# Turning the q of four attention layers with transposing DMAs in place of matmuls

## What is computed

```python
x = x + _L0_attn_ref(_layernorm(x), ...)               # a state space layer, "m" below
x = x + _L0_xattn_ref(_layernorm(x), ctx, ctx, ...)    # cross attention, 16 heads of 8, "x0"
x = x + _L0_ffn_ref(_layernorm(x), ...)                # latent attention, 16 heads of 4, "s0", then 8 experts, top 2
x = x + _L1_attn_ref(_layernorm(x), ...)               # self attention, 4 key heads, "s1"
x = x + _L1_xattn_ref(_layernorm(x), ctx, ctx, ...)    # cross attention with rotation, "x1"
x = x + _L1_ffn_ref(_layernorm(x), ...)                # gelu MLP, "f"
```

## Time and profile before

| | |
|---|---|
| median of 3 runs | 752.23 us (751.91 to 753.66) |
| the profiled execution | 759.68 us |
| its span, first to last instruction | 757.9 us |
| mean granted TensorE clock | 0.98 |
| PE busy | 650.6 us (86%), 5800 matmul records |
| DVE busy | 557.3 us (74%), 1513 |
| ACT busy | 436.7 us (58%), 861 |
| POOL busy | 178.8 us (24%), 348 |

### The profile page before, as it was taken

One profiled execution on the slowest core, in us unless ns is written; L12 is line 12 of the kernel. 1 busy time (PEld: TensorE's weight loads), 2 busy tenths in 40 slices (PEclk: granted clock), 3 DMA queues, 4 the chain that ended last, 5 costly groups with the idle time before them and its releaser, 6 DMA issues.

```text
span 757.9 us, 14898 instructions
## 1 busy us (share of the span) xinstructions
PE 650.6 (86%) x5800; PEld 428.1 (56%) x5800; DVE 557.3 (74%) x1513; ACT 436.7 (58%) x861; POOL 178.8 (24%) x348
## 2 busy tenths in 40 slices
PE   0787889899899898898988898888899799898877
PEld 0255448547555585456743585555567467584556
DVE  8549885847986679786787557789858875669683
ACT  0423565676577546756476543646775677657634
POOL 9332430203212022321131103232311301020102
PEclk9979999999999999999999998989999999999999
DMA  8110000000000000000000000000000000000000
GB/s 288 49 65 8 1 1 1 1 2 1 1 14 10 1 2 15 8 2 1 10 6 1 2 1 15 1 2 1 1 15 2 1 1 1 1 1 1 2 1 22
DMA packets 10358, 10.62 MB, mean 14 GB/s; under 512 B 2832, under 2 KB 9520, under 8 KB 10032
## 3 DMA queue, kind: packets, MB, share of 16 engines
q1 hardware_dynamic: 9568, 6.98, 3.1%
q10 hardware_dynamic: 720, 2.69, 0.9%
HBM read 8.60 MB, written 1.07 MB: 13 GB/s over the span
## 4 chain that ended last, share of the span: by engine, by line
PE 53%; DVE 30%; ACT 10%; issue 4%; POOL 2%; POOLq 0%; ACTq 0%; DVEq 0%
PE psA L1551 8%; PE psB L1538 7%; PE psO L1489 7%; DVE qs L1139 7%; ACT P L840 6%; PE psB L1465 5%; PE psA L1449 4%; PE psM L1428 4%; DVE QT L1127 3%; PE psM L1304 2%; DVE qs L1134 2%; PE psM L1347 2%; DVE spare L1113 1%; PE psO L1480 1%; ACT QT L837 1%
## 5 line engine op out<-in xcount | busy, mean ns | idle before, releaser
L840 ACT ACTIVATE P<-psB 128x512 f32<-128x512 f32 x320 | 177.8, 596 | 105.3 <-PE psB L1465 69.2
L1139 DVE TENSOR_REDUCE qs<-psA 128x2 bf16<-128x512 f32 x256 | 165.0, 689 | 25.0 <-PE psA L1449 23.7
L1449 PE MATMUL psA<-kz_s,QT 128*128 128x512 bf16 x256 | 91.8, 391 | 13.3 <-DVE qs L1139 6.3
L847 ACT ACTIVATE P<-psB,W 128x256 f32<-128x256 f32 x160 | 66.9, 472 | 49.5 <-PE psB L1538 42.1
L1465 PE MATMUL psB<-QT,kz_s 128*128 128x256 bf16 x512 | 86.7, 276 | 5.3 <-ACT QT L837 4.4
L1489 PE MATMUL psO<-P,vp 128*32 128x256 f32 x1024 | 81.7, 393 | 6.8 <-ACT P L840 4.7
L1428 PE MATMUL psM<-identb,qs 128*128 128x128 bf16 x896 | 72.6, 222 | 13.9 <-DVE qs L1115 5.9
L1428 PEld LDWEIGHTS psM<-identb,qs 128*128 128x128 bf16 x896 | 56.3, 99 | 39.6 <-issue 13.4
L1465 PEld LDWEIGHTS psB<-QT,kz_s 128*128 128x128 bf16 x512 | 39.7, 98 | 52.9 <-issue 31.1
L1127 DVE COPY QT<-psM 128x1024 bf16<-128x1024 bf16 (+1 forms) x80 | 52.5, 660 | 19.7 <-PE psM L1428 18.8
L1551 PE MATMUL psA<-w,P 128*128 128x128 f32 x512 | 65.7, 278 | 0.6 <-DVE x L1216 0.4
(11 more groups left out here) (178 smaller groups left out, 1128.3 us busy)
## 6 DMA issues: line engine op xcount, KB each, us to landing
w<-expert_w ACTq DMA_DIRECT2D x2, 1024.0 KB, 8.7
toep<-decay_rows SPq DMA_DIRECT2D x4, 512.0 KB, 5.8
x<-x SPq DMA_DIRECT2D x8, 128.0 KB, 2.8
y<-base SPq DMA_DIRECT2D x8, 128.0 KB, 1.9
W<-weights SPq DMA_DIRECT2D x1, 940.0 KB, 6.6
rows<-bias_rows SPq DMA_DIRECT2D x1, 872.0 KB, 7.6
ctxp<-context SPq DMA_DIRECT2D x8, 64.0 KB, 2.1
fw<-mlp_w ACTq DMA_DIRECT2D x2, 256.0 KB, 10.6
```

The lines of the kernel that those rows point to most:

```text
L840: act.activation(P[:, p, :, :].rearrange("p a s -> p (a s)"), psB[:, s.u % B_BANKS, :], ACT.Exp, scale=LAYERS[s.L]["scale"]).then_inc(b_dr ...
L847: ins = act.activation(P[:, p, f, :], psB[:, s.u % B_BANKS, f * S:f * S + S], ACT.Gelu, bias=bias[:, n:n + 1])
L1139: dve.tensor_reduce(qs[L["W"]][j][:, t * H + h:t * H + h + 2, 0], ps.rearrange("p (h c) -> p h c", h=2), AX.X, ALU.max, negate=True).then_ ...
L1449: ins = pe.matmul(ps, QT[j][:, h // L["HB"], t * 128:t * 128 + 128], kz[s.L][j][:, kv:kv + 2, :].rearrange("p h s -> p (h s)"), start=True ...
```

## The change

The steps Q and M leave PE, DVE and ACT, and become steps of SP alone. SP gets its own order string and its own waits. For each turn it waits for `q_split` (Q) or `a_drained` (M) and issues two DMAs with transpose=True, one for each 128 positions, straight from `qs` to `QT`: [128, 512] bf16 to [128, 4, 128] (in s0 [128, 256] to [128, 2, 128]). PE waits before the first A or S of a half for the semaphore `q_turned` of that slot and half. The context loads, stores and x loads stand in SP's string as well. The strings of the other four engines are new too.

```diff
     if s.kind in ("Q", "M"):
-        return ("PE", "ACT") if query_on_scalar(s) else ("PE", "DVE")
+        return ("SP",)
...
-        "00w0102010010w101000a1a01a01aaaawa101101b0b10w1b02bb00b00a0b000b0001a001aa100a1aa100aaa0xaaa10aa1aa211aa1a1b1a"
...
+        "w00w0010100011121002001w1aaaaawa20110001102bb0abbb000b00000101001020aa001aaa1baaa0xaaa1aaa11aa1a11a1a1a1xaa1a1"
...
+    "SP": (
+        "00aa11bb00awa11b22b00ccaa020a121abbcx0c11bb33d2d12cc33dd22cc44e3e3yd24d4ee33dd344e55ef66fgg4455eeff664gg77hh57"
+        "57hfhf66g7g7hh55f66fg77ghh567"
...
+    turns = {}
+    for s in order["SP"]:
+        if s.kind in ("Q", "M"):
+            turns[s.j, s.q] = turns.get((s.j, s.q), 0) + 16 * T
+            s.turn = turns[s.j, s.q]
...
+        def query_turn(s, t):
 
             groups = groups_of(s)
-            n = len(groups)
-            return QT[s.j][:, groups[0]:groups[0] + n, :].rearrange("p g s -> p (g s)"), bf(m)[:, 0:n * S]
+            n, hb = len(groups), LAYERS[s.L]["HB"]
+            h = t * H + groups[0] * hb
+            return (QT[s.j][:, groups[0]:groups[0] + n, t * 128:t * 128 + 128],
+                    qs[LAYERS[s.L]["W"]][s.j][:, h:h + n * hb, :].rearrange("p h w -> p (h w)"))
...
-            for s in order["DVE"]:
-                if s.kind == "C" and s.L == "x1" and s.q == 0 and s.b + 2 < B:
+            for s in order["SP"]:
+                if s.kind == "C":
...
+                if s.kind in ("Q", "M"):
+                    if s.kind == "Q":
+                        split = previous(s, "P3", s.L).after["q_split"]
+                        if ahead(q_split, split):
+                            sp.wait_ge(q_split, split)
+                    else:
+                        a = previous(s, "A", s.L, 2 * s.q + 1 if LAYERS[s.L]["cross"] else 8 * s.q + 7).a
+                        if ahead(a_drained, a + 1):
+                            sp.wait_ge(a_drained, a + 1)
+                    for t in range(T):
+                        turned, plain = query_turn(s, t)
+                        sp.dma_start(turned, plain, transpose=True).then_inc(q_turned[s.j][s.q], 16)
...
-                if s.kind in ("Q", "M"):
-                    m = filled(s)
-                    dst, src = query_block(s, m)
-                    dve.tensor_copy(dst, src).then_inc(misc_drained[m], 1)
...
-                    drained(previous(s, "M", s.L, s.q // 2 if L["cross"] else s.q // 8))
+                    turned(previous(s, "M", s.L, s.q // 2 if L["cross"] else s.q // 8))
```

More of the change, by code:

```diff
@@ L133, in engines @@
     if s.kind in ("Q", "M"):
-        return ("PE", "ACT") if query_on_scalar(s) else ("PE", "DVE")
+        return ("SP",)
     if s.kind == "C":
-        return ("PE", "DVE") if s.q else ("PE", "DVE", "POOL")
+        return ("PE", "DVE") if s.q else ("PE", "DVE", "POOL", "SP") if s.L == "x1" and s.b + 2 < B else ("PE", "DVE", "POOL")
     if s.kind == "F3":
@@ L139, in engines @@
     if s.kind == "H":
-        return ("PE", "DVE") if s.L == "s0" else ("PE", "DVE", "POOL")
+        return ("PE", "DVE") if s.L == "s0" else ("PE", "DVE", "POOL", "SP")
     if s.kind == "R1":
@@ new lines @@
+        "0000000011120221b00b20bb0b2bbb1010120021111111111222111011100120x222222032322122311113x11331132322y321cccc11cc"
+        "1cc23232y3y212222222223222323223243343333333333343233223322y42222434334432dddddd422dd3423344233333333334334433"
+        "4343354444444444454444344333333334544543eeee33e3eee4554346z464444454446544464444646556655z66z46644545545554444"
+        "5555555565555566556456446466666z646666766576675576776775ffff7777ffff557577775557577777777555776755555656777767"
+        "gggg5gggg5655676677666667h66hh6hh5hhh766766766665777777777775775777765666556755776767667775755656676777567"
@@ L190 @@
-        "7675676757"
+        "0w1200101w0001111x222000022011002311x33y111223334y322244423324445333533454665z64z45554666447777557767667575666"
+        "7775556677"
+    ),
+    "SP": (
+        "00aa11bb00awa11b22b00ccaa020a121abbcx0c11bb33d2d12cc33dd22cc44e3e3yd24d4ee33dd344e55ef66fgg4455eeff664gg77hh57"
+        "57hfhf66g7g7hh55f66fg77ghh567"
     ),
@@ L422, in decoder @@
         x_loaded = [sem(f"x_loaded{j}") for j in range(SLOTS)]
+        q_turned = [[sem(f"q_turned{j}_{half}") for half in range(2)] for j in range(SLOTS)]
         ot_drained = [sem(f"ot_drained{o}") for o in range(2)]
@@ L528, in _, with ahead @@
         def _(sp):
+            passed = {}
+            def ahead(semaphore, value):
+                new = passed.get(semaphore.name, 0) < value
+                passed[semaphore.name] = max(value, passed.get(semaphore.name, 0))
+                return new
             def load_x(b):
@@ L568, in _ @@
                     load_context(s.b // 2 + 1)
-                if s.kind == "H" and s.L == "f":
+                if s.kind == "H":
                     store(s)
@@ L1288, in drained, with turned @@
                     pe.wait_ge(misc_drained[m], c)
+            def turned(s):
+                if ahead(q_turned[s.j][s.q], s.turn):
+                    pe.wait_ge(q_turned[s.j][s.q], s.turn)
             def reuse(emptied, unit, banks):
@@ L1413, in _ @@
                     ins.then_inc(misc_filled[m], 1)
[L1414 to L1420, removed]
-                        if ahead(a_drained, a + 1):
-                            pe.wait_ge(a_drained, a + 1)
-                    m = take(s)
-                    HB = L["HB"]
-                    for i, g in enumerate(groups_of(s)):
-                        for t in range(T):
-                            h = t * H + g * HB
-                            ins = pe.transpose(bf(m)[:, i * S + t * 128:i * S + t * 128 + 128],
-                                               qs[L["W"]][j][:, h:h + HB, :], identb[:, :])
-                    ins.then_inc(misc_filled[m], 1)
                 if s.kind == "A":
@@ L1435, in _ @@
                         drained(previous(s, "K", s.L))
-                    drained(previous(s, "Q", s.L, s.q // 2 if L["cross"] else s.q // 8))
+                    turned(previous(s, "Q", s.L, s.q // 2 if L["cross"] else s.q // 8))
                     reuse(a_drained, s.a, A_BANKS)
```

52 lines of the change are left out of this document (18 added, 34 removed).

## The result

The changed kernel takes **781.42 us** (median of 4 runs, 780.84 to 783.81), the kernel before beside it 752.22: ratio 1.039, 95% interval 1.0365 to 1.0416. Forecast was 697 us, so the prediction is wrong, and in the direction too. These spans are some 6 to 8 us longer by that, and not by the turns.

What follows compares the result with a forecast made beforehand. PE was taken to bound the kernel: span 757.9 - 96.5 = 661.4 us, plus 0.75 x 55 of late turns = 702.7, less the 5.7 us profile offset = 697 us. Range 671 to 731, for 8 in 10 664 to 815.

Steps and rivals of the forecast that it cites:

- 72.6 + 13.9 + 10.0 = 96.5 us: Time leaving PE: turning matmuls 72.6 us, idle before them 13.9, waits of QT's readers for its copies 10.0.
- The copies counted as nothing: DVE loses 52.5 us and ACT 38.3 us of copies, priced at zero because PE work beside them hides them.
- The new order was priced only through the turns it covers: New PE order entered only as work between a half's last A and first S: median 4.2 us over 64 M turns.
- a sign of being wrong: Stated warning: if PE's waits for DVE and ACT grow instead of those for the DMA, the new order costs time.
- Turn 2.9 us, 0.45 us an issue: On SP: 2.4 us to land plus 0.5 for first issue and semaphore; issuing 256 DMAs at 0.45 costs 115 us.
- Rival 1: Transposing DMA slow to issue (1.2 us) or land, at the first S after M turns: turn 5.0 us, 809 us; chance 0.21.
- Rival 2: A turn's two transposing DMAs run one after another: turn 4.3 us, kernel 767 us; chance 0.15.
- Shortfall 55 us at 2.9, 100 at 3.6; three quarters count: Summed lateness of 64 M and 32 first Q turns against PE work between, by turn length; three quarters lengthens the span.
- the worked example: Batch 3, second cross layer, first half: PE work between last A and first S summed to 3.6 us.
- SP has room: SP's queue: issuing takes 256 x 0.45 = 115 us of the span, so capacity suffices, though a waiting turn holds up others.
- It decides at a turn of 4.0 us: Break-even: three quarters of a 129 us shortfall equals the 96.5 us saved, at a turn 1.1 us longer than assumed.
- The clock: Granted clock said to dip to 0.90 only in the first 50 us; short PE waits leave it 1.00, no loss priced.

Runs made afterwards that it cites:

- no_turn: Changed kernel with all 256 turning DMAs left out, QT zeroed once, PE waiting for the split q and drained A itself: 741.71 us, ratio 0.987.
- four_dmas: Changed kernel with each turn issued as four turning DMAs of half the size, 512 in all: 1045.84 us, ratio 1.3897.
- q_merged: Changed kernel with the two Q turns of a layer as two DMAs of twice the size, 192 DMAs instead of 256: 783.63 us, ratio 1.0409.
- old_order: Changed kernel with the engine order of the kernel before, Q and M struck out, all turns by DMA on SP: 902.99 us, ratio 1.199.
- filler: Changed kernel with eight matmuls on the identity matrix ahead of each new PE wait for a turn: 799.77 us, ratio 1.0632.

## Why the prediction was wrong

Step by step, with 752.2 us as the start (each figure a difference of medians): removing the turn work -20.7, the new order +10.2, a trip of 2.9 us through SP +0.5, the longer issue of the turning form +39.2; together 781.4. They add up by construction, so the sum proves nothing; and the zeroing of QT may shift some 3 us from the first term to the third, about -24 and +4.

1. **"72.6 + 13.9 + 10.0 = 96.5 us"**: the step that failed. It is 20.7. I took PE's busy 86% and its 53% of the chain as proof that PE time removed is span removed. Two things were wrong in it. The 72.6 us are not PE's alone: 24.0 of them lie under the records of other steps, so no more than 48.6 could go. And the idle time (13.9 + 10.0) did not go but moved: PE was only one of three in a ring, where A waits for the reduce and V for the exp, and without the transposes it waits 10.6 us longer before A and 11.5 before V.
2. **The copies counted as nothing**: DVE and ACT have 48 and 39 us less to do, and PE waits for them longer than before. No run took the copies away alone, so their own share is open.
3. **The new order was priced only through the turns it covers.** By itself it costs 10.2 us (measured without any turn), while PE waits for DVE and ACT. I had named that as a sign of being wrong, with no term in the sum.
4. **"Turn 2.9 us, 0.45 us an issue"**: the landing was right (2.5), the issue is 1.27, nearly three times the nearest row. Rival 1 named just this (1.2 us), so its mechanism came true, at 3.8 us a turn instead of its 5.0, because the landing is counted from the start of an issue and so includes that of the second DMA. Rival 2 fell: the second DMA of a turn is issued about 1.3 us after the first, before that has landed, and the median landing stays at 2.5 us. The idle time before S and A that rival 1 put above 100 us is 66.8 (29.7 + 17.1 + 11.1 + 8.9).
5. **"Shortfall 55 us at 2.9, 100 at 3.6; three quarters count"**: too much by far. It measured 0.5 us at 2.9 and 39.7 at 3.8, since my sum of PE time in between left out the waits in it. From the last reduce to the first reader I had a median of 4.2 - 1.3 = 2.9 us over the 64 M turns; in no_turn it is 4.1, and 6 of the 64 lie under 2.9. (In the worked example the last term is also too small: the T3 step is four records of 0.15 us, not two, so 3.9 us in place of 3.6.) With the true times the sums are 2 and 23; and queueing, which I had dismissed with "SP has room", takes 23 to 61. The 41.3 us of the forecast and the 39.7 measured are near by luck: two errors offset.
6. **"It decides at a turn of 4.0 us"**: with 20.7 in place of 96.5 even the 10 us of the order and 11 of waiting use up the gain. By my own sum a turn of 3.8 us would still have been faster; it is 3.9% slower.
7. **The clock**, priced at nothing, is 0.925 with 0.98 before. That it dips "only in the first 50 us" was a misreading: in the kernel before it is 0.81 from 455 to 473 us and 0.87 from 493 to 511 too. The part it has in the 39 us was not isolated; PE's longer busy time bounds it at some 17 us.

Put right, 697 + 75.8 (term 1) + 10.2 (term 3) - 1.6 (term 5) = 781.4 us.

By the Trainium skill ("Advanced Engine Details and Errata", X-Bar Transpose (TRN2)) a transposing DMA on trn2 is as fast as a regular one. For the landing the traces bear that out (2.5 against 2.3 us); for the issue on SP they don't (1.27 against 0.63 us).

## What to carry to other kernels

Busy time saved on an engine is worth time only up to the next wait in its ring, and the busy time of a group includes what lies under other records; before counting it, run the kernel with that work left out, in the unchanged order, for the most it can give. A trip through a DMA queue has two prices, its length against the work between source and reader, and its share of an in-order queue: sort that queue by when sources are ready, and compare its issue time with the spacing of the trips. Here nothing beats the kernel before by more than 0.3%: turns with long cover can be given to SP without loss, but not with a gain that is clear of the noise.

## What the runs showed that I had not expected

- Issuing one transposing DMA takes SP 1.25 to 1.27 us whether it moves 32 to 64 KB (four_dmas), 64 to 128 (changed) or twice that in the Q turns (q_merged); these are medians. A plain DMA to the same destination takes 0.63, a store or load 0.38 to 0.47.
- Where PE had more waits of a few microseconds the granted clock was lower, against what I wrote: mean 0.98 before, 0.925 changed, 0.847 in old_order, 0.787 in four_dmas, with PE idle for 14, 20, 26 and 32% of the span. In filler, where matmuls fill such waits, it is back at 0.957 with 18% idle. In the changed kernel's window from 50 to 100 us it is 0.76, so part of that stretch ran at 1.2 GHz:

```profile
50.00:100.00 50.00, 37.23 (x299) 23.34 (x288) 32.54 (x87) 16.57 (x35) 12.29 (x21) 0.76 0.32 53
```
